# A graph attention layer on one Trainium2 core: node groups of 2048 edges in place of tiles of 1024

## What is computed

```python
h_src, h_dst = x[src], x[dst]
e = leaky_relu(concat([h_src, h_dst, ef]) @ W_attn + b_attn, 0.01)[:, 0]
m = concat([h_src, ef]) @ W_ne
emax  = segment_max(e, dst, N)
ex    = exp(e - emax[dst])
denom = segment_sum(ex, dst, N)
z = segment_sum((ex / denom[dst])[:, None] * m, dst, N)
out = layernorm(x + relu(concat([x, z]) @ W_out))
```

## Time and profile before

| | |
|---|---|
| median of 3 runs | 4891.12 us (4876.2 to 4896.5) |
| the profiled execution | 4895.69 us, span of its instructions 4893.9 us |
| mean granted TensorE clock | 0.65 of full speed |
| busy share | PE 43%, DVE 53%, ACT 46%, POOL 70% |
| chain that ended last | issue 27%, another core or an unknown queue 23%, DVE 20%, DVEq 13%, ACT 11% |
| DMA | 628.94 MB in 759572 packets, mean 129 GB/s |

### The profile page before, as it was taken

How to read it: one execution, slowest core, us unless ns; L and a number is a source line. 1 busy time by engine, 2 the same in 40 slices (tenths; PEclk the granted TensorE clock), 3 DMA queues, 4 the chain that set the end, 5 groups by cost and what they waited for, 6 DMA issues and landing times.

```text
span 4893.9 us, 64908 instructions
## 1 busy us (share of the span) xinstructions
PE 2096.0 (43%) x10260; PEld 1948.9 (40%) x10261; DVE 2615.8 (53%) x4868; ACT 2270.5 (46%) x4123; POOL 3429.4 (70%) x3149
## 2 busy tenths in 40 slices
PE   0444444444444344443444444444444444444446
PEld 0434444433334334343433433343333334443436
DVE  5545555554555455554555555555545555555557
ACT  1545555544444444444444444444444445444444
POOL 6677776777777667777777767777677777777751
PEclk8666666666666666666666666666666666666666
DMA  5445444554555445444445444554444544544541
GB/s 113 129 124 142 123 132 128 136 132 129 130 133 137 119 130 134 133 134 130 130 132 139 130 122 127 137 134 130 132 128 130 141 130 129 130 130 131 137 124 52
DMA packets 759572, 628.94 MB, mean 129 GB/s; under 512 B 608412, under 2 KB 608796, under 8 KB 759332
## 3 DMA queue, kind: packets, MB, share of 16 engines
q1 hardware_dynamic: 646164, 519.51, 35.5%
q0 software_dynamic: 100096, 102.60, 12.6%
q10 hardware_dynamic: 13072, 4.80, 0.5%
HBM read 621.58 MB, written 4.81 MB: 128 GB/s over the span
## 4 chain that ended last, share of the span: by engine, by line
issue 27%; another core or an unknown queue 23%; DVE 20%; DVEq 13%; ACT 11%; ACTq 5%; PE 2%; POOL 0%
DVE u L625 5%; DVE e L694 5%; DVEq L749 3%; DVE prod L621 3%; ACT psS L498 2%; DVE acc L687 2%; ACT zs L507 2%; DVEq L716 2%; ACT zb L508 2%; ACTq L512 2%; ACT acc L470 1%; ACT pT L460 1%; DVEq L687 1%; DVE bounds L739 1%
## 5 line engine op out<-in xcount | busy, mean ns | idle before, releaser
L365 POOL DMA_INDIRECT V<-in_x_dram,srcs x3128 | 3404.1, 1088 | 1343.3 <-issue 907.5
L855 PE MATMUL psT<-ident,e 128*128 128x128 f32 x3136 | 824.4, 414 | 2739.2 <-DVE e L694 1642.7
L855 PEld LDWEIGHTS psT<-ident,e 128*128 128x128 f32 x3136 | 599.5, 217 | 2882.1 <-DVE e L694 1726.6
L861 PE MATMUL psG<-V,pT 128*128 x6288 | 1364.1, 390 | 0.0
L861 PEld LDWEIGHTS psG<-V,pT 128*128 128x128 f32 x6288 | 1314.5, 307 | 0.0
L460 ACT COPY pT<-psT 128x512 f32<-128x512 f32 x785 | 451.8, 576 | 1372.7 <-remote 1316.1
L621 DVE TENSOR_TENSOR prod<-V,wa 128x1024 f32<-128x1024 f32 x391 | 479.5, 1226 | 563.3 <-issue 563.2
L694 DVE TENSOR_TENSOR e<-zb,zs 128x1024 f32<-128x1024 f32 x392 | 480.4, 1226 | 491.2 <-remote 427.3
L735 DVE CUSTOM_DVE_ANT_0 um<-ubc,psS 128x1024 f32<-128x1024 f32 x391 | 477.3, 1221 | 129.8 <-ACT psS L498 99.3
L625 DVE TENSOR_REDUCE u<-prod 128x8 f32<-128x1024 f32 x391 | 477.0, 1220 | 51.1 <-issue 18.2
L508 ACT ACTIVATE zb<-um,ebias 128x1024 f32<-128x1024 f32 x391 | 442.9, 1133 | 0.0
(11 more groups left out here) (96 smaller groups left out, 620.9 us busy)
## 6 DMA issues: line engine op xcount, KB each, us to landing
ubc<-scores SPq DMA_DIRECT2D x391, 512.0 KB
dbc<-in_dst_dram SPq DMA_DIRECT2D x390, 512.0 KB
V<-in_edge_attr_dram SPq DMA_DIRECT2D x390, 256.0 KB
V<-in_x_dram,srcs POOLq DMA_INDIRECT x3128
scores<-u SPq DMA_DIRECT2D x391, 4.0 KB
srcs<-in_src_dram SPq DMA_DIRECT2D x390, 4.0 KB
out_dram<-y SPq DMA_DIRECT2D x12, 256.0 KB
xt<-in_x_dram ACTq DMA_DIRECT2D x6, 448.0 KB
```

What stands on the lines that cost most here:

```text
L365: nc.gpsimd.indirect_dma_start(V[0:n, s, j, 0:F], None, x[:, :], bass.IndirectOffsetOnAxis(ap=srcs[0:n, s, j:j + 1], axis=0)).then_inc(h_i ...
L855: last = nc.tensor.transpose(psT[:, i, j * P:(j + 1) * P], e1[:, :].rearrange("q (p j) -> q j p", j=J)[:, 4 * i + j, :], ident[:, :])
L861: last = nc.tensor.matmul(psG[:, bass.ds(bk, 1), 0:AW].rearrange("p a f -> p (a f)"), pT[:, i, j * P:(j + 1) * P], V[:, bass.ds(sv, 1), 4 ...
```

## The change

The unit of a round becomes a node group of DT = 2 x 1024 edges; there are NQ = 196 groups. The tiles of 1024 remain the unit of `V`, of the gathers and of the scores.

- **Round.** In a round ACT and DVE take the two tiles in turn through one psS: square, masked maximum, square, masked maximum. The leaky ReLU is now taken before the exponential: ACT writes `SLOPE * um + bias` into psS, DVE takes the maximum with `um + bias` (one input in PSUM), and ACT needs one Exp per edge in place of two. `weigh` and its pass over two SBUF tiles are gone. The bounds, `alpha`, `rescale` and `merge` are done once per group. LAG is 2.
- **Attention weights of the product.** `wa_v` is copied once into psM (PSUM), so the product of L621 has one operand in PSUM. As psM is written by PE as well in the first 7 turns, DVE waits there for `y_ready` and PE for `prod_done`.
- **TensorE.** Sixteen transposes and sixteen matmuls per round, the matmuls first; psT is 2 x 1024 wide, psG one buffer. Slots are returned in pairs by the sequencer after `agg_done`.
- **SyncE.** The dst loads are gone from its queue. For each pair of tiles it waits for the second masked maximum of the group two before (its count is kept in a register that adds up the windows), then spreads the scores of the group that comes next, stores those of the group after it (four rows of scratch in DRAM in place of two), loads `srcs` and the edge rows.
- **ScalarE's queue.** At the end of a group ACT issues the two dst loads of the next group, 512 KB each, and waits for both at that group's start.
- **GpSimd.** The gathers are the same 3128 instructions in the same order.

```diff
-LAG = 3
-BEHIND = 2
-AHEAD = 3
+LAG = 2
+AHEAD = 4
+Y_STEPS = (2, 1, 2, 1, 1)
...
-        wa_v = wa[:, :].rearrange("p (k f) -> p k f", f=F)[:, 0:3:2, :]
+        wa_v = psM[:, 0:2 * F].rearrange("p (k f) -> p k f", f=F)
...
+            def group_read(q):
+                count = sp.value_load(trip[0:1, bass.ds(2 * q + 1, 1)], min_val=1, max_val=NB)
+                sp.reg_add(read, read, count)
+                sp.wait_ge(um_done[1], sp.snap(read))
+
+            def pair(turn, i, q, odd, stored, last):
+                group_read(q - 2)
+                for h in range(2):
+                    spread_scores(stored, h, 2 - 2 * odd + h)
+                for h in range(2):
+                    store_scores(2 * q + h, 2 * odd + h)
...
+                for h in range(2):
+                    sp.wait_ge(v_free[2 * i + h], turn + (1 if i == RING // 2 - 1 else 0))
+                    load_ef(RING * turn + 2 * i + h, 2 * i + h)
...
+                    nc.scalar.activation(psS[:, :], dbc[:, 0, :], ACT.Square, bias=nbias[:, 0:1], scale=FAR).then_inc(sq_done[0], 1)
+                    act.wait_ge(um_done[0], G)
+                    nc.scalar.activation(psS[:, :], dbc[:, 1, :], ACT.Square, bias=nbias[:, 0:1], scale=FAR).then_inc(sq_done[1], 1)
+                    act.wait_ge(wn1, G)
+                    act.wait_ge(um_done[1], G)
+                    nc.scalar.activation(psS[:, :], um[:, 0:ST], ACT.Identity, bias=wnode[:, 4:5], scale=SLOPE).then_inc(low_done[0], 1)
+                    act.wait_ge(lr_done[0], G)
+                    nc.scalar.activation(psS[:, :], um[:, ST:DT], ACT.Identity, bias=wnode[:, 4:5], scale=SLOPE).then_inc(low_done[1], 1)
...
+                    rescale(G)
+                    weights_out(G, 0)
+                    weights_out(G, 1)
+                    for i in range(2):
+                        act.wait_ge(lr_done[i], G)
+                        nc.scalar.activation(e1[:, i * ST:(i + 1) * ST], um[:, i * ST:(i + 1) * ST], ACT.Exp, bias=nn[:, 0:1]).then_inc(e_done[i], 1)
...
+                if next_dst:
+                    act.wait_ge(sq_done[1], act.snap(g) - 1)
+                    for h in range(2):
+                        act.dma_start(dbc[:, h, :], edge_rows(dst, 2 * q + 2 + h).rearrange("(a e) -> a e", a=1).broadcast_to((P, ST))).then_inc(d_in[h], 16)
...
-                nc.vector.tensor_tensor(e1[:, :], zb[:, :], zs[:, :], ALU.max).then_inc(mx_done, 1)
...
+                    for h in range(2):
+                        dve.wait_ge(low_done[h], G)
+                        nc.vector.scalar_tensor_tensor(um[:, h * ST:(h + 1) * ST], um[:, h * ST:(h + 1) * ST], wnode[:, 3:4], psS[:, :],
+                                                       ALU.add, ALU.max).then_inc(lr_done[h], 1)
...
+                pe.wait_ge(pt[0], G)
+                pe.wait_ge(merged, G + 1)
+                multiply(0, sv)
+                pe.wait_ge(pt[1], G)
+                multiply(1, sv)
+                if turns:
+                    for i in range(2):
+                        pe.wait_ge(e_done[i], G + 1)
+                        turn(i)
```

More of the change, by code:

```diff
@@ L313, in _ @@
+            sp.wait_ge(trip_in, 16)
+            group_read(0)
+            for h in range(2):
+                spread_scores(1, h, 2 + h)
+            for h in range(2):
+                store_scores(4 + h, h)
             for s in range(AHEAD):
@@ L499, in supertile @@
-                    weights_out(G, 1)
-                    rescale(G)
-                    act.wait_ge(nn_done, G)
-                    nc.scalar.activation(ebias[:, :], wnode[:, :], ACT.Identity, bias=nn[:, 0:1], scale=-1.0).then_inc(ebias_done, 1)
-                    act.wait_ge(lowf_in, 16)
-                    act.wait_ge(ebias_done, G)
-                    nc.scalar.activation(alpha[:, bass.ds(act.snap(slots[0], min_val=0, max_val=LAG), 1), :].rearrange("p a k -> p (a k)"),
-                                         half[:, bass.ds(t, 1), :].rearrange("p a k -> p (a k)"), ACT.Exp, scale=ebias[:, 2:3])
```

469 lines of the change are left out of this document (240 added, 229 removed).

## The result

| | kernel before | changed kernel |
|---|---|---|
| median, beside each other (4 runs each) | 4890.84 us | 4959.08 us |
| range | 4876.2 to 4896.5 | 4951.9 to 4972.3 |
| ratio (95% interval) | | 1.0147 (1.0116 to 1.0179) |
| profiled execution, span | 4893.9 us | 4960.3 us |
| first and last um of a round, mean round | 72.8 to 4800.5, 12.1 us per 1024 edges | 89.5 to 4859.3, 24.0 us per 2048 |

The change is **slower by 1.5%**; the forecast was 4500 us. First the page of the changed kernel: busy time, and the chain that ended last.

What follows compares the result with a forecast made beforehand. The prediction took the kernel as paced by GpSimd's gathers plus its ring waits. 4895.7 us - 447 (less contention) + 55 (windows, start) = 4504, stated as 4500 us; range 4150 to 4860.

Steps and rivals of the forecast that it cites:

- Gathers: GpSimd's 3128 gathers: mean falls from 1.088 to 0.945 us, as VectorE's passes with two SBUF inputs go.
- The term of -447: Contention at GpSimd: 3128 gathers, each 0.143 us shorter, taken in full from the time, -447 us.
- its lower bound: If a PSUM operand did not help the product, only the max L694's part goes: 72%, or -320 us.
- The undisturbed round, 17.4 us for 2048 edges: Chain of ScalarE and VectorE, 7.3 + 10.1 us with the dst loads on its path, against 17.8 before.
- GpSimd's waiting at the ring ... I leave it: 2.0 us per group.: GpSimd's waits for ring slots, 1.0 us per tile before, kept unchanged: 22.0 us per group with 20.0 of gathers.
- double (slots are now returned in pairs): Bad end of the ring wait: it could double, as GpSimd then waits for a whole group.
- Rival 2: Slow rounds belong to the edges, not GpSimd's pace: 3.2 us per tile stay, 23.8 per group, 4840 us; chance 0.16.
- both of its signs: Signs of edge-bound slow rounds: GpSimd waits much more than 400 us, and long waits before pT stay.
- Rival 3: Dst loads start late, between second Exp and next square: about 5680 us, or 5070 milder; chance 0.12 for above 4916.
- Rival 1: GpSimd's waiting at the ring vanishes too, pace 20.0 us per group: 4110 us; chance 0.17.
- Windows, +55: Kernel's end and start: extra windows behind the last gather, output stage and two more products at the start, +55 us.

Runs made afterwards that it cites:

- experiment 6: Changed kernel unaltered on a new chip: 4159.6 us, 0.9255; with GpSimd memset pauses after every fourth gather 0.9523 (another chip 0.9900), after every second 0.9456.
- experiments 1 and 2: After ten tiles, no gathers: changed kernel 3824.9 us, kernel before 3843.7; changed kernel with half the gathers 3899.1, with plain SyncE loads instead 4077.4.
- experiments 3 and 4: Kernel before: release by wait 1.0022, plus PSUM weights 1.0139; changed, SBUF weights 1.0072. GpSimd waiting for landed gathers: changed 5148.0 us, 1.0055, 1.0148; before 1.0260.

## Why the prediction was wrong, point by point

- **Gathers.** Forecast 0.945 us and none of 1.9 us; measured 0.944. The term of -447 was -451, and it was right as a busy time. The split in its lower bound (72% for the max L694, from two gathers) was too uneven: over the whole trace it is 57% (259 of 451 us).
- **The undisturbed round, 17.4 us for 2048 edges.** Smooth rounds were 17.3 us; without gathers the median was 17.5. Right, and with the dst loads just on its path: in a round of the trace without gathers the pair was in 5.6 us after its issue (2006.13 to 2011.71 us), as reckoned. There their wait showed in 160 of 200 rounds, 2.9 us each, and VectorE then waited 1.3 us for the square in 177. In the working, 8.6 + 0.6 + 1.1 is 10.3 and not 10.1; nothing in the forecast hangs on it, since GpSimd's 20.0 us are longer.
- **"GpSimd's waiting at the ring ... I leave it: 2.0 us per group."** This is the step that failed: a wait kept at its old length while the gathers beside it were shortened. In the result it was 891 us, 4.5 us per group, where the forecast had 391. I had seen that everything moved 2.7 us after GpSimd's last gather and had read it as GpSimd pacing the others. The runs show in its place that hand-overs come late while gathers run without a gap, and mostly in GpSimd's stops (90% of the increments). The wait and the gathers were therefore not two terms that can be changed one at a time: taking 267 us from the gathers in the old kernel added 330 us to the stops.
- **Where the term's bounds stood.** The old kernel waited 176 times for a slot, 2.3 us each; the new one 177 times, 5.0 us each. I had named "double (slots are now returned in pairs)" as the bad end of this term. Doubled, 4.0 us per group, gives 4500 + 392 = 4890, above my range's upper end; I gave it no chance of its own (and the chances listed add up to 0.83 for faster and 0.12 for slower, not 0.82 and 0.13). The cause is not the pairs alone, since the old kernel with single slots and the weights in PSUM lost as much.
- **Rival 2** (4840) was by its number one of the two nearest, beside the milder form of rival 3 (5070), and both of its signs came: GpSimd waited 891 us, and long waits before pT stayed (361 us). But its ground is wrong: the slow rounds vanish with the gathers, the edges being the same. **Rival 3** had the right side, and its sign was there too: idle time before nbias of 1143 us in 200 rounds, 5.7 each. But 769 of it is "issue", the late queue; without gathers the wait for the dst loads is 2.3 us a round and the round 18.2. So most of the sign was an effect of the lateness.
- **Rival 1** (the waiting vanishes, 4110 us): in experiment 6 this is what happened, 4159.6 us. That this lies in the range is luck: the range was worked out from 4896 us for the kernel before, which took 4492.6 there, and rival 1 by its ratio would be 0.84, where 0.9255 was measured.
- **Windows, +55.** Behind the end of the last gather lie 182 us now, 144.7 before: +37.

Summed by its measured terms: 4895.7 - 451 (gathers) + 491 (slots) + 20 (issue) - 31 (waits for srcs) + 37 (end) = 4962, and the profiled execution took 4962.2. This is a count of GpSimd's own time; it closes whatever the cause, and shows where the time went, not why.

## What to carry to other kernels

Before counting a shorter instruction on the pacing engine as time won, look at what ends its waits: if everything moves on only after that engine has stopped, its busy time and its waits move together, and the rest of the kernel may live on its stops. The sign to look for is a wait by "remote" or "issue" whose producer was done long before and which ends at nearly the same moment on several engines. And time such a change more than once and on more than one chip: the same pair of kernels gave 1.0147 and 0.9255.

## What the runs showed of the hardware that I had not expected

- While GpSimd issued a gather every 1.25 us, completions of TensorE reached the other engines in the median only 1.7, 3.0 and 5.2 us after the last of 8, 16 and 32 gathers in a row (the first with a pause after each tile, the others in the changed kernel). ScalarE waited up to 19.3 us for such a hand-over.
- Register, branch and semaphore instructions of three other engines took about 0.70 us in such stretches, 755 of them: 2 of 3090 were that slow beside the first five gathers of a row, 16% beside the thirteenth to sixteenth. It does not depend on the gathers' bytes (a quarter of them: a wait of 933 us), and as many bytes by SyncE's plain loads don't cause it (20 such instructions).
- The kernel before took 4885 to 4970 us in six of seven measurements and 4493 us in one. The lateness was in every trace of full gathers from five of the six (the one of experiments 1 and 2 has no such trace of its own), and absent in the seventh (none of 12262 such instructions over 0.6 us; the kernel before has no trace there). The granted clock differs too, 0.652 against 0.677 over the whole span, but the smooth parts run at equal lengths in both: um 1221 ns, a gather 944 ns.
- One chip served in two measurements, of experiments 3 and 4, and the kernel before took 4884.9 and 4959.4 us there. So 1.5% can lie between measurements on one chip, and comparisons across them are only that sure. The chip free of lateness was used once: whether it is the chip or the occasion that is free of it isn't shown.
- **Open:** what the gathers and the completions share, why it drains at the rate it does, and what made one measurement free of it. No run here reaches that. A ring with more slots, or groups of 4096 edges, which might carry one stop over more edges, wasn't tried.
